# Probabilities times values in a gated cross-attention kernel: one matmul over both halves of the values, the halves summed afterwards

## What is computed

```python
x = x + tanh(g_xattn) * xattn(layernorm(x), ctx, mask)
x = x + tanh(g_ffn) * ffn(layernorm(x))

def xattn(h, ctx, mask):
    h = rmsnorm(h)
    q, k, v = h @ wq.T, ctx @ wk.T, ctx @ wv.T          # 16 heads of 32
    p = softmax(where(mask, q @ k.T * 32**-0.5, -inf))
    return sigmoid(h @ wg.T) * ((p @ v) @ wo.T)

def ffn(h):                                             # hidden width 1408
    gate, up = h @ w_gate, h @ w_up                     # 4-bit weights times scales
    y = (silu(gate) * up) @ w_down
    return y / sqrt(mean(y*y) + eps)
```

## Time and profile before

| | |
|---|---|
| median of 3 runs | 613.23 us (610.06 to 613.46) |
| the profiled execution, whole time | 612.71 us |
| its span, first to last instruction | 610.4 us |
| mean granted TensorE clock | 0.968 of full |
| PE busy | 569.5 us (93%) |
| DVE busy | 468.5 us (77%) |
| ACT busy | 325.9 us (53%) |
| POOL busy | 226.0 us (37%) |
| first and last matmul of `attend` | 37.8 us and 348.3 us |

### The profile page before, as it was taken

The page is one execution under the profiler, slowest core; times in us unless marked ns, Lnnn a source line. Parts: engine busy times, 40 slices in busy tenths (PEclk is TensorE's granted clock), DMA queues, the critical chain, the costliest instruction groups (busy, mean ns, idle before and its releaser), DMA issues.

```text
span 610.4 us, 12518 instructions
## 1 busy us (share of the span) xinstructions
PE 569.5 (93%) x4154; PEld 498.4 (82%) x4154; DVE 468.5 (77%) x1063; ACT 325.9 (53%) x872; POOL 226.0 (37%) x244
## 2 busy tenths in 40 slices
PE   2799999999999999999998989989999999999996
PEld 2699889888898888988887766877988888899983
DVE  6666989869897677895666988898898799877721
ACT  4666465434554334652346734756666666766620
POOL 6811130001300011200002643866866776777630
PEclk9886999999998998997999989999999999999999
DMA  7920145432453223332455005702001210111011
GB/s 233 330 86 1 55 144 173 142 100 74 143 172 130 81 84 110 97 128 88 161 190 196 2 23 177 270 1 79 34 1 37 78 36 2 34 36 35 35 62 31
DMA packets 27899, 59.38 MB, mean 97 GB/s; under 512 B 3656, under 2 KB 5832, under 8 KB 27848
## 3 DMA queue, kind: packets, MB, share of 16 engines
q1 hardware_dynamic: 27848, 58.76, 29.2%
HBM read 39.62 MB, written 19.14 MB: 96 GB/s over the span
## 4 chain that ended last, share of the span: by engine, by line
PE 55%; DVE 24%; issue 9%; POOL 6%; ACT 5%; DVEq 1%; DMA 0%; SPq 0%; ACTq 0%; POOLq 0%
PE bank L1697 14%; PE bank L1710 11%; PE bank L317 10%; PE bank L1549 6%; PE bank L1601 4%; PE bank L1553 3%; PE bank L1577 3%; POOL hT_lo L753 2%; DVE nmax L1122 2%; DVE part_gate L1324 2%; DVE vb_lo L1090 2%; PE bank L326 2%; DVE stats L1107 2%; DVE pT_lo L1127 2%; DVE hidden L1339 1%
## 5 line engine op out<-in xcount | busy, mean ns | idle before, releaser
L1697 PE MATMUL bank<-mT_hi,wgu 128*128 128x320 f32 x440 | 139.9, 328 | 14.2 <-DVE part_up L1324 4.9
L1697 PE MATMUL bank<-mT_lo,wgu 128*128 128x320 f32 x440 | 132.0, 310 | 0.0
L872 ACT ACTIVATE probs<-bank,nmax 100x96 f32<-100x96 f32 x256 | 66.4, 343 | 87.6 <-DVE nmax L1122 87.6
L1697 PEld LDWEIGHTS bank<-mT_hi,wgu 128*128 128x128 f32 x440 | 82.9, 188 | 30.0 <-DVE part_up L1324 8.0
L1697 PEld LDWEIGHTS bank<-mT_lo,wgu 128*128 128x128 f32 x440 | 83.2, 189 | 3.5
L760 POOL TENSOR_TENSOR part_gate<-part_gate 128x320 f32<-128x320 f32 x55 | 57.1, 1038 | 76.9 <-DVE part_gate L1324 76.9
L959 ACT ACTIVATE part_up<-bank,scale 128x320 f32<-128x320 f32 x110 | 57.3, 522 | 46.8 <-PE bank L1697 46.8
L1324 DVE SCALAR_TENSOR_TENSOR part_up<-bank,scale,part_up 128x320 f32<-128x320 f32 x110 | 58.3, 545 | 19.5 <-ACT part_up L959 17.6
L959 ACT ACTIVATE part_gate<-bank,scale 128x320 f32<-128x320 f32 x110 | 52.2, 528 | 28.7 <-PE bank L1697 27.9
L766 POOL TENSOR_TENSOR part_up<-part_up 128x320 f32<-128x320 f32 x55 | 57.1, 1039 | 22.9 <-DVE part_up L1324 21.2
L1324 DVE SCALAR_TENSOR_TENSOR part_gate<-bank,scale,part_gate 128x320 f32<-128x320 f32 x110 | 55.3, 542 | 12.0 <-ACT part_gate L959 10.5
(11 more groups left out here) (145 smaller groups left out, 1465.0 us busy)
## 6 DMA issues: line engine op xcount, KB each, us to landing
gate_up_scratch<-left SPq DMA_DIRECT2D x12, 512.0 KB, 6.4
down_scratch<-left SPq DMA_DIRECT2D x12, 512.0 KB, 3.9
wgu<-gate_up_scratch SPq DMA_DIRECT2D x11, 512.0 KB, 6.1
words<-in_packed SPq DMA_DIRECT2D x18, 256.0 KB
xn<-in_x SPq DMA_DIRECT2D x16, 200.0 KB
xa<-in_x SPq DMA_DIRECT2D x16, 200.0 KB
x_scratch<-gate SPq DMA_DIRECT2D x16, 200.0 KB
ctx_raw<-in_ctx_tail SPq DMA_DIRECT2D x4, 768.0 KB, 8.0
```

Of the source, the lines that this page charges most:

```text
L872: last = nc.scalar.activation(probs[i % 2][:, cols], SC[i % HPG][0:L, cols], ACT.Exp, bias=nmax[:, i % 4, b:b + 1])
L1697: last = nc.tensor.matmul(product_bank(j, t, i, k)[:, 0:TG], wgu[t][:, k, 128 * i:128 * i + 128], mT[j % 2][half][:, k, :], start=half == ...
```

## The change

`vb_hi` and `vb_lo` become one tile, `vb_both`, with the halves as its second dimension. In `attend` each chunk now has two matmuls in place of three: `pT_hi` against both halves of the values at once (136 columns, the `hi` part into columns 0 to 135 of bank 7 and the `lo` part from column 256 on, `PV_LOW`), and `pT_lo` against `vb_hi` (68 columns). Six matmuls with six weight loads replace nine.

The two parts of the result must be added. ACT gets `attn_low`: behind `pT_hi` of a step it waits for the `attend` of the step before and copies the 100 x 136 lower part to SBUF. DVE's `attn_norm` becomes `attn_sum`: wait for that copy, reciprocal as before, a sum of 100 x 136 (PSUM plus the copy) into one of two new tiles `pv_sum`, and the product, which now reads `pv_sum` in SBUF. PE's next `attend` waits for the sum (`s_pvsum`) and no longer for the product; job T still waits for the product.

Beside it three things move in the text: POOL's four `weight_lo("wo", k)` go from ahead of its steps 0 to 3 to right behind each of them, POOL's first five feed-forward tiles into its steps 11 to 15, and the rest of them follows `AT_LAST`; in these steps POOL has no other work, so the order of its instructions stays. Three small tiles are new (544 bytes per partition each), and the scratch for software DMAs is cut to 8192 bytes; the kernel issues none.

```diff
-        vb = [sb(phase_a, f"vb_{half}", [128, CHUNKS, 2, HEADS * VW], F32R) for half in ("hi", "lo")]
+        vb_both = sb(phase_a, "vb_both", [128, 2, CHUNKS, 2, HEADS * VW], F32R)
+        vb = [vb_both[:, half] for half in range(2)]
...
+        pv_low = sb(phase_a, "pv_low", [L, NB * VW], F32)
+        pv_sum = [sb(phase_a, f"pv_sum{s}", [L, NB * VW], F32) for s in range(2)]
...
+            def attn_low(g, i):
+
+                n = STEPS * g + i
+                act.wait_ge(s_pv, n + 1)
+                if not isinstance(n, int) or n:
+                    act.wait_ge(s_pvsum, n)
+                nc.scalar.activation(pv_low[:, :], PV[0:L, PV_LOW:PV_LOW + NB * VW], ACT.Copy).then_inc(s_pvlow, 1)
+
             def step(g, i, last=False):
                 probsT_hi(g, i)
+                if not isinstance(g, int) or g or i:
+                    attn_low(*last_step(g, i))
                 for ahead in step_ahead(g, i):
                     exp_step(*ahead)
...
-            def attn_norm(g, i):
+            def attn_sum(g, i):
+
                 n, hg, h = STEPS * g + i, i // HPG, i % HPG
+                dve.wait_ge(s_pvlow, n + 1)
                 pv = PV[0:L, 0:NB * VW].rearrange("t (b w) -> t b w", w=VW)
-                dve.wait_ge(s_pv, n + 1)
                 nc.vector.reciprocal(rinv[:, i % 4, :].unsqueeze(2), pv[:, :, HD:HD + 1]).then_inc(s_inv, 1)
+                nc.vector.tensor_tensor(pv_sum[i % 2][:, :], PV[0:L, 0:NB * VW], pv_low[:, :], ALU.add).then_inc(s_pvsum, 1)
+                total = pv_sum[i % 2][:, :].rearrange("t (b w) -> t b w", w=VW)
                 dve.wait_ge(s_inv, n + 1)
-                nc.vector.tensor_tensor(o[hg % 2][:, :, HD * h:HD * h + HD], pv[:, :, 0:HD],
+                dve.wait_ge(s_pvsum, n + 1)
+                nc.vector.tensor_tensor(o[hg % 2][:, :, HD * h:HD * h + HD], total[:, :, 0:HD],
                                         rinv[:, i % 4, :].unsqueeze(2).broadcast_to([L, NB, HD]), ALU.mult).then_inc(s_on, 1)
...
                 if not isinstance(n, int) or n:
-                    pe.wait_ge(s_on, n)
-
+                    pe.wait_ge(s_pvsum, n)
+
+                both = PV[0:L, :].rearrange("t (a w) -> t a w", a=2)
                 for c in (0, 2, 1):
-                    for p, (ph, vh) in enumerate(PASSES):
-                        last = nc.tensor.matmul(PV[0:L, VW * c:VW * c + 2 * VW].rearrange("t (b w) -> t b w", w=VW), pT[i % 2][ph][:, c, :],
-                                                vb[vh][:, c, :, VW * i:VW * i + VW], start=c == 0 and p == 0, stop=c == 1 and p == 2)
+                    cols = slice(VW * c, VW * c + 2 * VW)
+                    nc.tensor.matmul(both[:, :, cols].rearrange("t a (b w) -> t a b w", w=VW), pT[i % 2][HI][:, c, :],
+                                     vb_both[:, :, c, :, VW * i:VW * i + VW], start=c == 0, stop=False)
+                    last = nc.tensor.matmul(both[:, 0, cols].rearrange("t (b w) -> t b w", w=VW), pT[i % 2][LO][:, c, :],
+                                            vb[HI][:, c, :, VW * i:VW * i + VW], start=False, stop=c == 1)
                 last.then_inc(s_pv, 1)
```

More of the change, by code:

```diff
@@ L220, in build @@
         s_pv, s_inv, s_on = sem("attn_ready"), sem("inverse_ready"), sem("attn_normed")
+        s_pvlow, s_pvsum = sem("attn_low_copied"), sem("attn_summed")
         s_gate, s_gated, s_x1 = sem("gate_ready"), sem("gated_ready"), sem("x1_ready")
@@ L448, in build @@
         SETUP = 8
+        PV_LOW = 256
         FJ, FO = bank[0], bank[1]
@@ L715, in step @@
                         mask_bias(g + 1)
+                if last and i in FIRST_AT:
+                    ffn_tile(0, FIRST_AT[i])
             def weight_lo(name, k):
@@ L741, in _ @@
                   .then_inc(s_split["wk"], 1)
-            for k in range(KT):
-                weight_lo("wo", k)
             def ffn_rstd(j):
@@ L799, in _ @@
                     step(0, i)
+                    if i < KT:
+                        weight_lo("wo", i)
                 with pool.Fori(0, GROUPS - 1) as g:
@@ L806, in _ @@
                     step(GROUPS - 1, i, True)
-                for t in range(FT):
-                    ffn_tile(0, t)
+                for part_of in AT_LAST:
+                    if isinstance(part_of, int):
+                        ffn_tile(0, part_of)
                 rest()
             with pool.Else():
+                for k in range(KT):
+                    weight_lo("wo", k)
                 with pool.Fori(0, B) as b:
@@ L1027, in _ @@
                 for part_of in AT_LAST:
-                    if part_of == "T3":
+                    if part_of == "H":
+                        attn_low(GROUPS - 1, STEPS - 1)
+                    elif part_of == "T3":
                         job_hi(GROUPS, "T3")
@@ L1162, in step @@
                 if not isinstance(g, int) or g or i:
-                    attn_norm(*last_step(g, i))
+                    attn_sum(*last_step(g, i))
                 if i % HPG == SCORES_AT:
@@ L1410, in _ @@
                     if part_of == "H":
-                        attn_norm(GROUPS - 1, STEPS - 1)
+                        attn_sum(GROUPS - 1, STEPS - 1)
                     elif part_of == "T3":
@@ L1856 @@
     from concourse.bass_utils import run_bass_kernel_spmd
-    nc = bacc.Bacc("TRN2", target_bir_lowering=False, num_devices=1)
+    nc = bacc.Bacc("TRN2", target_bir_lowering=False, num_devices=1, dynamic_dma_scratch_size=8192)
     arrays, args = {}, []
```

## The result

The changed kernel takes 621.44 us (median of 4 runs, 620.88 to 626.86); the kernel before, measured beside it, 611.64 us (609.35 to 613.46). The ratio is 1.018, with an interval of 1.011 to 1.025: slower by some 10 us. I had forecast 616.3 us, a loss of 3.1 us on the 613.2 that I started from; 9.8 us were measured. So the sign was right and two thirds of the size were missed. The time lies just inside the range given, 608 to 622. The profiled execution has a span of 619.7 us against 610.4.

What follows compares the result with a forecast made beforehand. Two engines take turns: PE paces from step 2 to 6 and in the last group, DVE from 6 to 10 and 14 to 2. 3.9 - 1.35 + 0.5 = +3.1 us on 613.2 gave 616.3 us, range 608 to 622.

Steps and rivals of the forecast that it cites:

- PE's term: Attention on PE: six matmuls 0.089 us apart instead of nine, 0.53 us for 0.80, a gain of 0.27 us.
- My sign of an error there: Attention matmuls: a first one 0.12 or 0.18 us behind its neighbour would show the gain forecast for PE wrong.
- the forecast's -1.35: Last group from step 6, where PE is busy throughout: five attentions, -1.35 us.
- DVE's term: DVE's attention pass, reciprocal to next instruction: 0.63 us instead of 0.41, 0.22 us more per pass.
- ACT's and POOL's terms: ACT's copy takes 0.35 us, hidden; POOL's SBUF work delays DVE's product by 0.5 us, once a cycle.
- POOL's hold: DVE's product, now with both inputs in SBUF, stands until POOL's instruction ends: 0.5 us more, once in each cycle.
- The sum of a cycle: Step 6 to 10 +0.66, 10 to 14 +0.35, 14 to 2 +0.88, 2 to 6 -1.08; with POOL's 0.5, +1.31 us.
- My +0.5 beside the feed-forward tiles: Last group: DVE makes about two passes without idle time beside the feed-forward tiles, +0.5 us.
- a rival with one or two falls more: Longer PE waits, fewer matmuls: one more fall of TensorE's clock 618.5 us, two 620.2 or more; chance 0.16.
- the rival of dearer hand-offs: DVE's sum costs 0.39 us more per pass (621.4 us), or the 136-column matmul takes 0.12; chance 0.17.

Runs made afterwards that it cites:

- e9_filled_fully: Changed kernel plus 24, 13 and 13 unread matmuls ahead of attend at steps 10, 14 and 2: 610.04 us, ratio 0.995.
- e7_no_copy: Changed kernel without ACT's copy; DVE waits for PE's matmuls and adds a tile of zeros: 619.80 us, ratio 1.016.
- e10_before_filled: Kernel before plus 7, 3 and 5 unread matmuls ahead of attend at steps 10, 14 and 2: 605.32 us, ratio 0.988.
- e3_filled_waits: Changed kernel plus 16, 10 and 10 unread matmuls ahead of attend at steps 10, 14 and 2: 615.32 us, ratio 1.007.
- e1_matmuls_only: Changed kernel with its six matmuls but without ACT's copy and DVE's sum, lower part missing from the result: 603.77 us, ratio 0.986.
- e2_sum_only: Changed kernel with nine matmuls instead of six, copy, sum and waits kept: 626.34 us, ratio 1.026.

## Why the prediction was right, and where it was wrong

**PE's term was right.** 0.27 us per attend was forecast; 0.71 became 0.48 us first to last start, and with a pair at 0.177 the six cost 0.53, as reckoned. My sign of an error there was a bad one: the matmul behind the 136 columns does start 0.125 later, and the narrow one makes up for it. The window from step 6 to 10 of the last group, where PE is busy all the time, went from 19.57 to 18.42 us between the starts of the two blocks of scores: -1.15 for four attentions, where 4 x 0.27 is 1.08. The fifth of the forecast's -1.35 stands behind this window.

**DVE's term was nearly right.** 0.26 us per pass against 0.22. The 0.04 is a start 0.07 later of the product behind the sum, less the 0.03 by which the sum is shorter; ahead of that product two waits now stand.

**ACT's and POOL's terms.** ACT's copy measured 0.28 for my 0.35 and is hidden. All 64 copies end ahead of their reciprocal. POOL's hold exists and is 0.31 us at 173.68 (0.60 for 0.29) where I had 0.5. Without clock falls the stretch from 10 to 14 is 16.45 us in e9_filled_fully against 16.05 before, +0.40 in all, where I had put down +0.35 for the passes and +0.5 for POOL. How the 0.40 divides between the two is not shown.

**The sum of a cycle came out right, with luck.** Between the starts of the blocks of scores, where no fall disturbs: step 6 to 10 went from 19.94 to 20.98 us, +1.04 (forecast +0.66); 10 to 14 +0.40 (forecast +0.85); 14 to 2 from 17.44 to 18.45, +1.01 (+0.88); 2 to 6 from 23.67 to 22.61, -1.06 (-1.08), the second and fourth taken from e9_filled_fully. In all +1.4 where I had +1.31, but the first stretch is 0.4 dearer than forecast and the second 0.4 cheaper, and the two errors cancel. In the first, three passes were counted: from its first reciprocal to `oT_lo` DVE takes 0.78 us more, which is three times 0.26, and it begins that reciprocal 0.26 later than before (0.88 us behind the start of the scores, where it was 0.62). Three cycles make +4.2, and with the last group +3.0, against the +4.7 between the two filled kernels.

**The steps outside the cycles.** The first six steps and all behind the last scores moved by 0.1 us each. They don't test the terms: the first six steps took 39.8 us before, 39.7 after, 36.8 in e7_no_copy and 43.5 in e10_before_filled, with 7 to 17 us at the lower level. These differences don't follow the changes made, each time is from one execution, and I take them as scatter. My +0.5 beside the feed-forward tiles can't be seen in it.

**The step that failed is the one on TensorE's clock.** The sum gave such falls nothing. The three cycles grew by 10.4 us (from 239.1 to 249.5), of which +4.2 is the trade; the other 6.2 us are falls of the granted clock: 34 us at the lower level in place of 17. I had the mechanism, "both falls come behind a stretch in which PE waits for DVE", and left it out of the sum, as a rival with one or two falls more at a chance of 0.16. The trace of before let one see more: PE waited 0.4 to 0.7 us (in the table's measure) ahead of nine blocks of scores and the clock fell behind three of them. The sum itself made those waits longer: DVE needs up to 0.9 us more in a stretch and PE 1.1 less. They became 2.3, 1.3 and 1.3 us, and falls stood behind 8 of 9. The waits at steps 14 and 2 grew by less than the two terms together, since part of PE's saving turned into waits elsewhere in the stretch (0.93 us ahead of a transpose, L1616, where it was 0.43). What I priced at 0 to 4 us as chance was a consequence of my own terms. What a fall costs I had about right: 1.6 us from step 10 to 14 (18.02 against 16.45), with 3.4 us at the lower level; with 6.8 us it was 3.1 from step 2 to 6 in the kernel before (26.79 against 23.67). Filling the waits removes falls and loss together (e3_filled_waits, e9_filled_fully), with the number of matmuls raised, and filling helps the kernel before as well. So PE's idle time is a cause here and not only a companion. But a fill both shortens the wait and gives PE more to do; the same matmuls at a place without a wait were not tried, so these runs don't separate the two.

The Trainium skill, TensorE: Matmul & The Clock Gate, section "A second HAM failure mode: psum-queue depth-cycling", describes a kernel in which PE pauses briefly but often between groups of matmuls and its clock swings between the two levels. That is the rule which I should have weighed. The runs agree: with waits of 1.3 us or more ahead of the blocks of scores the clock fell behind 8 of 9, and in e9_filled_fully matmuls that nobody reads brought the stretch from 10 to 14 back from 0.91 to 1.00.

**A misreading and a coincidence.** The prediction says that all four blocks of scores start on a release by DVE. Three of the four in a cycle do: the block of step 6 starts without a wait, 0.19 us behind the last `attend` matmul, and the fourth wait of the earlier trace rows belongs to step 10 of the next cycle. And the rival of dearer hand-offs, a sum that costs 0.39 us more per pass, gave 621.4 us, the time measured. That is luck: a pass costs 0.26 more and the 136-column matmul nothing, so its mechanism is not there.

**What stays open.** How long a wait has to be for a fall is not settled. By the table the falls rise with the wait, but e1_matmuls_only waits 3.6 us per cycle and has 4 falls, e2_sum_only 3.4 and 8. Each count is from one execution, but the clocks of all executions say the same (0.967 to 0.983 against 0.952 to 0.958), so the wait ahead of the scores is not all that counts; what else does is open. It also isn't settled why the last falls of the filled kernels all stand behind step 2, where PE idles for another 0.4 us inside the block of scores; filling that wait wasn't tried.

## What to carry to other kernels

Where two engines take turns, a trade of work from the one to the other pays only in the stretches in which the relieved engine sets the pace: cut the trace there, price each stretch with its own sign, and make the change in those alone. Then ask what the remaining idle time of TensorE does to its clock: if the granted clock already falls behind short waits, a change that lengthens them can bring more falls (here 1.6 us for each 3.4 us at the lower clock), and that belongs into the sum. A handful of unread matmuls in a wait that can't be removed is a cheap test of it, and here also a gain (6.3 us of 611.6 in the kernel before).

## What was not expected of the hardware

Falls of the clock stood behind waits of PE of 0.4 to 2.5 us ahead of the scores, and filling waits of half a microsecond or less in the kernel before gained 6.3 us. Pairs of 136 and 68 columns run at 0.125 and 0.052 us, while their weight loads of 100 columns start 0.088 apart as before: the pair takes the time of two loads, 0.177 us, and doubling the columns of one matmul cost nothing. And DVE needs 0.10 us from the sum's end to the start of the product that depends on it and on the reciprocal, where a product behind the reciprocal alone started after 0.03; whether the second wait or the kind of input makes the difference is not shown.
